# One kernel, two layers: the first layer's modulated rows in two buffers with their norms beside the key sums, and one convolution tap and the second layer's first norm on ACT

## The reference, cut to what matters

```python
h = _layernorm(x) * (1 + ca) + sa
x = x + ga * _L0_attn_ref(h, ...)      # norms h again, then q, k, v, gate; softmax over key sums q^T k
h = _layernorm(x) * (1 + cb) + sb
x = x + gb * _L0_ffn_ref(h, ...)       # shared gated MLP, and 2 of 8 experts for each token
h = _layernorm(x) * (1 + ca) + sa      # second layer
x = x + ga * _L1_attn_ref(h, ...)      # W_in, causal convolution of 4 taps, silu, selective scan, gate, W_out
h = _layernorm(x) * (1 + cb) + sb
x = x + gb * _L1_ffn_ref(h, ...)       # gated MLP with two hidden layers of 1024
```

## Time and profile before

| | us |
|---|---|
| median of 3 runs | 2558.83 (2557.65 to 2562.32) |
| profiled execution, its own time | 2549.51 |
| its span, first to last instruction | 2547.7 |
| PE busy | 2278.8 (89%) |
| DVE busy | 1745.6 (69%) |
| ACT busy | 1376.8 (54%) |
| POOL busy | 1336.5 (52%) |
| mean granted clock of PE | 0.945 |

### The profile page before, as it was taken

How to read it: one execution, slowest core, us unless ns; L and a number is a source line. 1 busy time by engine, 2 the same in 40 slices (tenths; PEclk the granted TensorE clock), 3 DMA queues, 4 the chain that set the end, 5 groups by cost and what they waited for, 6 DMA issues and landing times.

```text
span 2547.7 us, 27225 instructions
## 1 busy us (share of the span) xinstructions
PE 2278.8 (89%) x8584; PEld 1482.8 (58%) x8584; DVE 1745.6 (69%) x2791; ACT 1376.8 (54%) x1822; POOL 1336.5 (52%) x1152
## 2 busy tenths in 40 slices
PE   7798999999999876789989989989998998998978
PEld 3576666766767532245655655655655654655666
DVE  6446455455454578997797797797797798687730
ACT  3143442533525364467757757666666766766622
POOL 4225143252342254666765755855766756667733
PEclk9799999999999998899989999999999998999989
DMA  7254556544554564445645745644645645546623
GB/s 251 64 164 155 168 170 200 166 143 139 159 163 153 165 188 120 132 127 147 184 116 142 197 116 144 186 120 141 181 128 148 180 127 152 161 125 178 170 76 91
DMA packets 253774, 384.52 MB, mean 151 GB/s; under 512 B 19168, under 2 KB 160112, under 8 KB 253632
## 3 DMA queue, kind: packets, MB, share of 16 engines
q1 hardware_dynamic: 223408, 281.07, 38.2%
q0 software_dynamic: 30224, 101.73, 13.0%
HBM read 345.67 MB, written 47.55 MB: 154 GB/s over the span
## 4 chain that ended last, share of the span: by engine, by line
PE 60%; DVE 15%; issue 11%; ACT 7%; POOL 6%; DMA 1%; DVEq 0%; POOLq 0%; SPq 0%; ACTq 0%
PE bank L235 25%; PE bank L1582 8%; PE bank L241 8%; PE bank L242 8%; DVE bank L1504 3%; DVE w_st L1512 3%; POOL d_in L1494 3%; PE bank L1107 2%; POOL f1L L1660 1%; DVE cv L1322 1%; PE bank L1784 1%; PE bank L1785 1%; PE bank L764 1%; PE bank L766 1%; PE bank L765 1%
## 5 line engine op out<-in xcount | busy, mean ns | idle before, releaser
L1494 POOL TENSOR_TENSOR d_in<-u,bc 128x512 f32<-128x512 f32 x512 | 659.0, 1296 | 364.4 <-DMA bc<-bc_rows 299.1
L1504 DVE TENSOR_TENSOR_SCAN bank<-bank,d_in 128x512 f32<-128x512 f32 x512 | 625.6, 1222 | 97.4 <-ACT bank L1560 65.9
L1582 PE MATMUL bank<-w_st,ident 128*128 128x512 f32 x1024 | 540.0, 643 | 87.0 <-DVE w_st L1512 86.6
L1560 ACT ACTIVATE bank<-dt,a_neg 128x512 f32<-128x512 f32 x512 | 348.3, 689 | 440.5 <-DVE w_st L1512 439.1
L1512 DVE TENSOR_TENSOR w_st<-bank,bc 128x512 f32<-128x512 f32 x512 | 344.6, 673 | 121.6 <-PE bank L1582 121.3
L241 PE MATMUL bank<-f1H,w_ring 128*128 128x512 f32 x768 | 359.0, 467 | 53.1 <-ACT raw L1391 24.0
L1582 PEld LDWEIGHTS bank<-w_st,ident 128*128 128x128 f32 x1024 | 196.3, 201 | 306.9 <-DVE w_st L1512 178.0
L242 PE MATMUL bank<-f1L,w_ring 128*128 128x512 f32 x768 | 309.9, 404 | 0.0
L241 PE MATMUL bank<-f0H,w_ring 128*128 128x512 f32 x512 | 230.7, 451 | 3.9 <-POOL f0L L1660 3.5
L1660 POOL TENSOR_TENSOR f0L<-mid,f0H 128x512 fp32r<-128x512 f32 x128 | 170.0, 1328 | 111.0 <-DVE f0H L1688 81.8
L241 PEld LDWEIGHTS bank<-f1H,w_ring 128*128 128x128 f32 x768 | 150.3, 196 | 130.8 <-issue 79.5
(11 more groups left out here) (213 smaller groups left out, 3970.7 us busy)
## 6 DMA issues: line engine op xcount, KB each, us to landing
bc<-bc_rows SPq DMA_DIRECT2D x256, 512.0 KB, 5.0
w_ring<-w_units POOLq DMA_DIRECT2D x160, 512.0 KB, 4.2
w_exp<-L_ffn_ew SPq DMA_DIRECT2D x240, 256.0 KB, 4.4
eo_rows<-eo SPq DMA_DIRECT2D x56, 256.0 KB, 4.2
xs<-xs_rows SPq DMA_DIRECT2D x24, 512.0 KB, 4.0
w_units<-h_T SPq DMA_DIRECT2D x16, 512.0 KB, 6.7
xA<-L_attn_x SPq DMA_DIRECT2D x8, 512.0 KB, 5.8
x_mid<-xA SPq DMA_DIRECT2D x8, 512.0 KB, 2.8
```

The source lines that it names most:

```text
L1494: pool.tensor_tensor(d_in[:, nth(b, s) % IN, :], u[:, c, :], rows_tile(b, use)[:, 0, :], ALU.mult).then_inc(in_made.sem, 1)
L1504: dve.tensor_tensor_scan(bank[:, :], bank[:, :], d_in[:, nth(b, s) % IN, :], 0.0, ALU.mult, ALU.add).then_inc(scanned.sem, 1)
L1560: act.activation(state_bank(b, s)[:, :], dt[:, c, :], ACT.Exp, scale=a_neg[:, c, n:n + 1]).then_inc(dA_made.sem, 1)
L1582: pe.matmul(y_bank(c)[:, :], ident[:, :], w_st[:, nth(b, s) % WG, :], start=False, stop=(n == NST - 1)).then_inc(summed.sem, 1)
```

## The change

- `h_tok` becomes two buffers, used in turn. norm1 is applied into `h_tok` rather than `xhatA`, and the modulation works in place. The waits change accordingly: norm1 waits for `x1` of batch b - 2, norm2 for the turn of `xhatA` of batch b - 1.
- The statistics and applications of both norms get places 23 to 35 lower (`stats1` 27.2 to 50, `norm1` 22.6 to 46.9, `stats2` 14 to 43.8, `norm2` 6.6 to 41.8). Seen from batch b - 1 they stand at +18.2 to +26.4, beside its key sums. POOL's reciprocal roots and SP's loads of x and rows move likewise. The x of batch 1 is loaded in the setup.
- The output of the shared feed-forward, `f_tok`, becomes one buffer instead of two. The modulation rows of the second layer, which lay in it during setup, go to `e_buf`.
- Other places of the first layer change: key sums on PE 15.3 to 13.5, `wo` 26.4 to 24.9, `gated` 23 to 16.7, `s_mul` 41.6 to 40.4, `route` 41.3 to 36, `r_sig` 40.9 to 52.7, `combine` 8 to 8.7, `xs_in` 4.5 to 2.9, `units_in` new, and a few more.
- Second layer: DVE makes only `minus_mean` (four numbers for each partition), and ACT applies the norm with four Identity instructions at place `xhat_act` = 34.8. ACT also makes the convolution's unshifted tap, right behind its copy of `raw`, and DVE adds the other three.

```diff
-PLAN = dict(
+PLAN = dict(xhat_act=34.8,
...
-    x_in=31.3, rows_in=48.6, rates=37.1, stats1=27.2, norm1=22.6, stats2=14, norm2=6.6, q_mul=7.1, q_add=9.2,
-    sim=15.3, sim_max=14.7, sim_exp=16.5, gated=23, wo=26.4, wo_add=26.2, f_stats=29.8, f_rstd=36.7, f_norm=34.7,
-    f_turn=38, fT=39.4, router=40, r_sig=40.9, route=41.3, shared=37.1, s1_act=24.6, s_mul=41.6, rank=43.2,
-    slots=43.9, s2=51.2, s2_out=50.6, scatter=48.5, xs_in=4.5, w_list=5, w_first=7.5, w_second=-1.6, xsT=0.3,
-    e_act=1.2, eo_out=9.9, gather=3, combine=8, x_out=10, experts=(6, 10, 12.2, 17, 20, 22.4, 25.5, 28, 33.5, 36))
+    units_in=56.2, rstd1=49, rstd2=39, rows_first=-46, rows_l0=-1, parts_high=3, parts_low=1.5, rows_l1=13.4,
+    rows_turn=23.0, n_low=-0.1, unit=7.0, stretch=1.87, after=72.0, last=55.2, last_gap=2.4, turn=68.2, x_in=53.1,
+    rows_in=62, rates=37.1, stats1=50, norm1=46.9, stats2=43.8, norm2=41.8, q_mul=7.1, q_add=9.2, sim=13.5,
+    sim_max=15.4, sim_exp=15.0, gated=16.7, wo=24.9, wo_add=26.2, f_stats=29.9, f_rstd=36.7, f_norm=34.7, f_turn=38,
+    fT=39.4, router=39.4, r_sig=52.7, route=36.0, shared=37.1, s1_act=25.7, s_mul=40.4, rank=43.2, slots=43.9,
+    s2=51.2, s2_out=51.8, scatter=48.5, xs_in=2.9, w_list=5, w_first=7.5, w_second=-1.2, xsT=0.3, e_act=1.2,
+    eo_out=9.9, gather=3, combine=8.7, x_out=14, experts=(6, 10, 12.2, 17, 20, 22.4, 25.5, 28, 33.5, 36))
...
             def att_vector(b):
-                x, x1 = xA[b % 3], x1_at(b)
+                x, h_tok, x1 = xA[b % 3], h_toks[b % 2], x1_at(b)
...
-                if b:
-                    dve.wait_ge(*n_turned.all(b - 1))
-                norm_apply(norm1, b, x, xhatA)
+                if b >= 2:
+                    dve.wait_ge(*x1_made.all(b - 2))
+                norm_apply(norm1, b, x, h_tok)
...
-                dve.tensor_tensor(h_tok[:, :, :], xhatA[:, :, :], row_of(b, CA).broadcast_to([P, TT, D]), ALU.mult
+                dve.tensor_tensor(h_tok[:, :, :], h_tok[:, :, :], row_of(b, CA).broadcast_to([P, TT, D]), ALU.mult
                                   ).then_inc(h_step.sem, 1)
...
                 yield x1 - PLAN_A["norm2"]
+                if b:
+                    dve.wait_ge(*n_turned.all(b - 1))
                 norm_apply(norm2, b, h_tok, xhatA)
...
             def att_pool(b):
-                yield x1 - 23
+                yield x1 - PLAN_A["rstd1"]
                 norm_rstd(norm1, b)
-                yield x1 - 11
+                yield x1 - PLAN_A["rstd2"]
                 norm_rstd(norm2, b)
...
                     act.wait_ge(*s2_done.at(b, n + 1))
-                    if b >= 2:
-                        act.wait_ge(*x2_made.all(b - 2))
-                    act.activation(pair_of(f_tok[b % 2], n), bank_pair(ffn.bank["s2", b, n]), ACT.Copy).then_inc(s2_out.sem, 1)
+                    if b:
+                        act.wait_ge(*x2_made.all(b - 1))
+                    act.activation(pair_of(f_tok, n), bank_pair(ffn.bank["s2", b, n]), ACT.Copy).then_inc(s2_out.sem, 1)
...
             def front_vector(b):
...
                 if b:
-                    dve.wait_ge(*h_made.all(b - 1))
-                norm_apply(normB, b, xB, xhatB)
+                    dve.wait_ge(*xhat_made.all(b - 1))
+                dve.wait_ge(*normB.rstd_made.all(b))
+                dve.scalar_tensor_tensor(out=minus_mean[:, :], in0=normB.stat[:, :, 0], scalar=-1.0, in1=normB.rstd[:, :], op0=ALU.mult,
+                                         op1=ALU.mult).then_inc(normB.step.sem, 1)
...
-                    dve.tensor_scalar(o, r[:, 0:S], conv_w[:, 0, c:c + 1], None, ALU.mult).then_inc(tap_made.sem, 1)
-                    for tap in range(1, KC):
-                        yield F + PLAN["conv"] + PLAN["raw_gap"] * c + PLAN["tap_gap"] * tap
-                        dve.wait_ge(*tap_made.at(b, c * KC + tap))
+                    for tap in range(TAPS):
+                        yield F + PLAN["conv"] + PLAN["raw_gap"] * c + PLAN["tap_gap"] * (tap + 1)
+                        if tap:
+                            dve.wait_ge(*tap_made.at(b, c * TAPS + tap))
+                        else:
+                            dve.wait_ge(*last_tap.at(b, c + 1))
                         dve.scalar_tensor_tensor(out=o, in0=r[:, tap:tap + S], scalar=conv_w[:, tap, c:c + 1], in1=o,
                                                  op0=ALU.mult, op1=ALU.add).then_inc(tap_made.sem, 1)
...
             def front_scalar(b):
+                yield F + PLAN["xhat_act"]
+                act.wait_ge(*normB.step.all(b))
+                if b:
+                    act.wait_ge(*dt_made.all(b - 1))
+                for t in range(TT):
+                    i = act.activation(xhatB[:, t, :], xB[:, t, :], ACT.Identity, bias=minus_mean[:, t:t + 1], scale=normB.rstd[:, t:t + 1])
+                i.then_inc(xhat_made.sem, 1)
...
                     act.activation(raw[:, c % 2, PAD:], shared.bank["raw", b, c][:, :], ACT.Copy).then_inc(raw_made.sem, 1)
+
+                    act.wait_ge(*raw_made.at(b, c + 1))
+                    if c == 0:
+                        act.wait_ge(*b_turned.all(b))
+                    act.activation(cv[:, c % 2, :], raw[:, c % 2, PAD:], ACT.Copy, scale=conv_w[:, TAPS, c:c + 1]).then_inc(last_tap.sem, 1)
...
             def front_tensor(b):
                 yield F + PLAN["turn"]
-                pe.wait_ge(*normB.step.all(b))
+                pe.wait_ge(*xhat_made.all(b))
```

More of the change, by code:

```diff
@@ L304, in adaln_kernel @@
             xhatA = sb("xhatA", [P, TT, D])
-            h_tok = sb("h_tok", [P, TT, D])
+            h_toks = [sb(f"h_tok{i}", [P, TT, D]) for i in range(2)]
             nT = sb("nT", [P, KD, S])
@@ L334, in adaln_kernel @@
                             .rearrange("p (k n) -> p k n", k=KD) for tile in (vg_T, qk_tok))
[L335 to L337 removed]
+            c_tok, c_act = (xhatF[0:B, 2 * i:2 * i + 2, :] for i in range(2))
+            sgn, mag = (s_tmp[0:B, i, :].rearrange("b (l d) -> b l d", l=2) for i in range(2))
+            rows = [tile[:, 0:NMOD * D] for tile in (f_both[0:B, :], e_buf[0:B, :, :, :].rearrange("b i j s -> b (i j s)"))]
             w_hid = w_exp[:, 0:2, :, :].rearrange("p w k d -> p (w k d)").rearrange("p (k n) -> p k n", k=KD)
@@ L476, in setup_scalar @@
                         act.wait_ge(mod_made.sem, 1 + 3 * l + c + 1)
-                        act.activation(rows[:, l, c * 512:(c + 1) * 512], banks[1 + 3 * l + c][0:B, :], ACT.Copy).then_inc(rows_made.sem, 1)
+                        act.activation(rows[l][:, c * 512:(c + 1) * 512], banks[1 + 3 * l + c][0:B, :], ACT.Copy).then_inc(rows_made.sem, 1)
             def parts_scalar():
@@ L507, in rows_tensor @@
                     for j in range(NMOD * KD):
-                        i = pe.transpose(bank[:, j * B:(j + 1) * B], rows[:, l, j * P:(j + 1) * P], ident[0:B, 0:B])
+                        i = pe.transpose(bank[:, j * B:(j + 1) * B], rows[l][:, j * P:(j + 1) * P], ident[0:B, 0:B])
                     i.then_inc(modT_turned.sem, 1)
@@ L521, in modulation_vector @@
                 for which in (CA, CB):
-                    r = rows[:, l, which * D:(which + 1) * D]
+                    r = rows[l][:, which * D:(which + 1) * D]
                     dve.tensor_scalar(r, r, 1.0, None, ALU.add).then_inc(mod_step.sem, 1)
@@ L525, in modulation_vector @@
                 for which in (GA, GB):
-                    r, s, m = rows[:, l, which * D:(which + 1) * D], sgn[:, l, :], mag[:, l, :]
+                    r, s, m = rows[l][:, which * D:(which + 1) * D], sgn[:, l, :], mag[:, l, :]
                     dve.wait_ge(mod_step.sem, done)
@@ L1275, in front_sync @@
                 if b:
-                    sp.wait_ge(*normB.step.all(b - 1))
+                    sp.wait_ge(*xhat_made.all(b - 1))
                 else:
```

47 lines of the change are left out of this document (19 added, 28 removed).

## The result

| | us |
|---|---|
| kernel before, median beside the changed one | 2558.24 (2549.68 to 2562.32) |
| changed kernel, median of three runs | 2520.56 (2519.48 to 2522.81) |
| ratio, with its 95% interval | 0.9859 (0.9832 to 0.9887) |
| profiled execution before, its own time and span | 2549.51, 2547.7 |
| profiled execution after, its own time and span | 2522.81, 2521.1 |

What follows compares the result with a forecast made beforehand. PE was taken to set the pace, except DVE in a 66 us stretch of a second-layer batch. First layer 17 + 4 and second layer 4 made 25 us off the 2558.8 us median: 2534, range 2505 to 2552.

Steps and rivals of the forecast that it cites:

- Line 1107: Last shared feed-forward product, first-layer batches 1 to 6: third s_act product ahead of the adding, ending 4.3 us earlier.
- The clock's share: At line 1107, PE's lower clock after the new 1.0 us wait: 0.9 us lost, bounds 0 and 1.8.
- Key sums: First layer, where the norms go: gelu waits behind maximum, exponential and table load, mostly covered; 0.6 us lost a batch.
- The 2.8 a batch: First layer, batches 1 to 6: 4.3 - 0.9 - 0.6 us gained each, 17 us in six.
- Transfers: First layer: SP issues the next batch's x, gate and modulation rows earlier; mostly hidden, counted as nothing.
- Batch 0: First layer: PE's 3.47 us wait for batch 1's second norm before line 230 goes; 4 us gained, bounds 3.5 and 5.3.
- Second layer: Front of batch 1, with no silus beside it, gains 4 us; six fronts count 0, batch 0's front is hidden.
- The step on ACT's queue: Second layer: ACT normalises ahead of the first two silus, which start 3.1 us later; the decay behind comes 3.0 late.
- the six fronts: Second-layer fronts that run under a scan: 0 gained each, bounds 4.4 us gained and 3.8 lost.
- The tap's side: Second-layer fronts: first tap's 2.64 us gone, second and third save 0.5 each, the third copy pushes a decay by 0.7.
- The norm's side: Second-layer fronts: DVE gains 1.2 us, loses 3.0 at the scan, gets about 0.6 back in the casts.
- The shared port: Second layer: a remaining DVE tap may take over the wait; six fronts lose 2.6 us each, sum 9 us, 2550.

Runs made afterwards that it cites:

- Experiments 8: Kernel before with only s_mul moved to 40.4, combine to 8.7 and x_out to 14: 2587.8 us, ratio 1.0113.
- 10: Kernel before with s_mul at 40.4, combine at 8.7, x_out at 14 and route at 36: 2558.0 us, ratio 1.0016.
- experiment 1: All first-layer edits of the change on the kernel before, PLAN and the second layer as before: 2532.1 us, ratio 0.9877.
- experiment 2: Only the second layer's edits (norm's application and unshifted tap on ACT) on the kernel before: 2555.2 us, ratio 0.9957.
- experiment 3: Changed kernel with the second layer's norm applied by DVE again, the unshifted tap staying on ACT: 2510.6 us, ratio 0.9794.
- experiment 9: Changed kernel with the second layer's norm far ahead for batches 1 to 7, root at 10, minus_mean at 11.4: 2506.5 us, ratio 0.9819.
- experiment 6: Changed kernel with the second layer's norm on ACT at 31.9 instead of 34.8 and minus_mean at 31.5: 2515.9 us, ratio 0.9823.
- 11: Changed kernel run again with no edit: 2521.6 us, ratio 0.9875 to the kernel before.

## Why the prediction was right, and where it was not

**Line 1107.** Right: 12 records, a wait of 1.13 (forecast 1.0), the other 20. The clock's share was 7.33 - 7.07 = 0.3 and not 0.9. A batch without the router's dip went from 102.7 to 99.5 us, 3.2 against the forecast 2.8; the five full batches between them gained 14.1 us in the profiled pair, 2.8 each.

**Key sums.** The new wait is there, ACT's `e_buf` in the row of waits: 5.1 in seven, of which 3.6 belong to the last batch and stood there before. The other six are some 0.24 each; I had 0.6.

**The 2.8 a batch is partly luck.** Line 1107 with its wait went from 12.33 to 8.46 us, 3.9, where I had 4.3 - 0.9 = 3.4, and the key sums took 0.24 and not 0.6. That would be 3.6. What brought it back to 2.8 is the clock at the router, which I had not in the sum: over these five batches it is at its lower level there for some 14 us before and 20 after, and at half the speed that costs at most half of the difference, 3.4 us in all. And the sum was made on a profiled execution of before that was fast by its clock, so it fits the profiled pair (26.6) much better than the medians (36 to 38), which it misses by 11 to 13 us.

**Transfers.** I counted nothing for the earlier loads. PE does not wait for `w_exp` in the first part, and behind the division for 3.2 us where it was 2.8.

**Batch 0.** The mechanism was right, the size too small. From one end of line 1107 to the next it went from 111.5 to 101.7 us. Line 1107 itself accounts for 3.9 of it (8.83 + 3.50 against 7.33 + 1.13), and the `xhatA` wait for the other 6 where I had 4 (bounds to 5.3). The products behind the wait had lost more clock than line 1107 does. The first fence is before, the second after:

```profile
123.29 9.55 PE L235 MATMUL bank<-w_qk,nT 128*128 128x512 f32 x16 [0.87 <-ACT nT L706]
```

```profile
117.55 1.04 PE L229 MATMUL bank<-ident,xhatA 128*128 128x128 f32 x8
119.74 7.13 PE L234 MATMUL bank<-w_qk,nT 128*128 128x512 f32 x16 [1.15 <-ACT nT L707]
```

2.4 us there, and 0.5 at the turn.

**What I said of the places was incomplete.** I credited the swap of the third product and the adding, and called the other places moves without effect or cover. With `s_mul` at 40.4 a `route` left at 41.3 would stand behind the first product; its move is what keeps the order. Experiments 8 and 10 show that the swap alone costs 24 to 29 us and that with the router's place added it is worth nothing. In the change it stands beside the move of the norms, and the first layer gains. No run moves the norms without the swap, and none parts them from the other places of the first layer, so how the gain divides among these is not shown.

**Second layer.** The sum of 4 us agrees with the traces: 3.1 in the profiled pair, 3.8 between the means of four traces each. The runs are less sure: by the ratios the changed kernel is 0.5 to 5 us ahead of experiment 1, by the medians 11, and experiment 2 has 7 to 15. The step on ACT's queue stands too: 3.17 us late for silus, decay and scan where 3.1 was forecast, four instructions in 2.08 us where 1.9 was. Experiments 3 and 9 show that it is what uses up the relief: with the norm elsewhere the second part is 14 and 17 us shorter (and 7 in experiment 6). Whether the 4 us come from the front of batch 1, as I put it, is not shown: from the end of line 1107 to the end of that front's `xp` product it is 155.3 before and 152.2 after, but 158.6 in experiment 1 and 159.3 in 11.

My own prices for the six fronts did not quite add up to the 0 that I took. The tap's side, 2.64 + 0.5 + 0.5 - 0.7 = 2.9 a front, was right: experiment 3 against 1 has 20.4 us in the second part, which is six fronts and the one of batch 1. The norm's side was 1.2 - 3.0 + 0.6 = -1.2 a front, and measures -2.3 (1690.7 - 1676.8 over six); with it the sum is near the 0. What I had named and not priced is PE's turn, which now waits for the silus' banks:

```profile
1476.06 1.41 PE L229 MATMUL bank<-ident,cv 128*128 128x128 f32 x8 [2.07 <-ACT mid L1738]
```

Behind it PE's products of line 241 take 0.63 us each, where experiment 3 has 0.40 at the same place and no such wait. That this is the missing microsecond is argued, not shown.

**The shared port.** The rival in which a remaining tap takes over the long wait did not come. The groups of the three remaining taps, before and after, and what the change put on ACT:

```profile
L1322 DVE SCALAR_TENSOR_TENSOR cv<-raw,conv_w,cv 128x512 f32<-128x512 f32 x96 | 102.1, 1064 | 0.4
```

```profile
L1324 DVE SCALAR_TENSOR_TENSOR cv<-raw,conv_w,cv 128x512 f32<-128x512 f32 x96 | 99.5, 1038 | 3.5 <-ACT cv L1405 3.2
...
L1405 ACT ACTIVATE cv<-raw,conv_w 128x512 f32<-128x512 f32 x32 | 23.2, 724 | 1.0
...
L1380 ACT ACTIVATE cv<-xB,minus_mean,normB_rstd 128x256 f32<-128x256 f32 x32 | 16.6, 590 | 9.6 <-DVE minus_mean L1311 9.6
```

They are no longer than before. One tap a front still takes 3.1 us (3.10 at 1503.51), and the one at the same place did before (3.14 at 1531.41).

My reading of the tap on DVE, 1055 ns on average, was too coarse. The numbers behind the count are least, middle and greatest ns, and under them is POOL beside the 2.64 us of the earlier trace rows:

```profile
L1318 DVE TENSOR_SCALAR cv<-raw,conv_w x32: 467/486/3233, 849.4 to 2137.1; 128x512 f32<-128x512 f32 x32
```

```profile
1509.95 2.53 POOL L1494 TENSOR_TENSOR d_in<-u,bc 128x512 f32<-128x512 f32 x2
```

The middle one takes 0.49 us, less than ACT's 0.72; six take 2.6 us or more. So for one instruction the row bears out the rule of the Trainium skill (ScalarE: Activation LUTs, Rules for kernel authors), which gives additions and multiplications to VectorE and not ScalarE. For the kernel it does not hold here: by experiment 3 the tap is worth more on ACT. For the norm it holds at the places 34.8 and 35.6; far ahead, in experiment 9, ACT is as good as DVE.

## What to carry to other kernels

An operation that is moved to an idle engine is paid for by what stands behind it in that engine's queue, and behind its reader in the next; give it the place where that engine already waits, and check the places of the operations that feed it as well. A swap of two places is judged with everything that stands between them: here the same swap cost 24 to 29 us, gave nothing, or was part of a change that gave some 30, with the router's and the norms' places moved as well. And a place called "without effect" has to be compared with the new places of the others, not with their old ones.

## What was not expected of the hardware

Two executions of the same code for the first seven batches differ by 8.8 us (750.7 and 759.5), and PE's clock was at its lower level for longer in the slower one. In the changed kernel PE is idle for 1.10 us ahead of the router's 16 products with 8 columns both in batch 3 and in batch 4, yet they take 3.15 us in the one, with the clock at its lower level from there on for 6.8 us, and 1.95 in the other, where it does not fall. And a multiplication of 512 columns by one number for each partition takes 0.72 us on ACT in every case and on DVE 0.47 to 3.23: mostly it is much cheaper there, and the long ones made it dear on average.
